# Query features kept in PSUM, groups placed two slots after their sums, one PSUM bank for all placements

## The reference

```python
xn = layernorm(x)
x = x + segment_sum(edge_weight[:, None] * xn[src], dst) @ gnn_W + gnn_b   # 100000 edges
      + linear_attention(xn) @ Wp + bp                                     # q, k = elu(.) + 1, 8 heads
x = x + adaptive_ffn(layernorm(x))        # weights merged from 8 experts by a gate, then a layer norm
```

## Time and profile before

| | us |
|---|---|
| median of 3 runs | 1649.34 (1647.26 to 1649.66) |
| the profiled execution | 1655.24 |
| its span, first to last instruction | 1653.3 |

### The profile page before, as it was taken

One profiled execution on the slowest core, in us unless ns is written; L12 is line 12 of the kernel. 1 busy time (PEld: TensorE's weight loads), 2 busy tenths in 40 slices (PEclk: granted clock), 3 DMA queues, 4 the chain that ended last, 5 costly groups with the idle time before them and its releaser, 6 DMA issues. The chain is left out here.

```text
span 1653.3 us, 27434 instructions
## 1 busy us (share of the span) xinstructions
PE 1478.6 (89%) x8552; PEld 652.4 (39%) x8552; DVE 1148.2 (69%) x2243; ACT 706.1 (43%) x1143; POOL 893.6 (54%) x883
## 2 busy tenths in 40 slices
PE   4988889999999999999999999989986999888995
PEld 2544333333333333434444444434433444543331
DVE  7978545565655655578888888868876666346777
ACT  4777533333333333224333343333335667424443
POOL 1003177777777777767777777777772444100000
PEclk9999989999999999979999999999997999999997
DMA  7899688888888888767777777777776335426674
GB/s 230 290 323 332 229 257 263 259 256 251 258 253 262 258 260 285 240 183 219 223 227 224 234 228 225 224 249 228 218 204 204 154 152 206 146 101 209 229 234 152
DMA packets 163487, 379.44 MB, mean 229 GB/s; under 512 B 26437, under 2 KB 32215, under 8 KB 163363
## 3 DMA queue, kind: packets, MB, share of 16 engines
q0 software_dynamic: 62720, 205.57, 40.9%
q1 hardware_dynamic: 99923, 171.27, 30.0%
q10 hardware_dynamic: 720, 1.06, 0.2%
HBM read 300.77 MB, written 78.23 MB: 229 GB/s over the span
## 5 line engine op out<-in xcount | busy, mean ns | idle before, releaser
L1083 POOL DMA_INDIRECT rows<-y_rows,idxT x516 | 515.7, 999 | 178.4 <-issue 166.8
L1417 DVE SCALAR_TENSOR_TENSOR acc<-bank,maskt,acc 128x512 f32 x392 | 275.8, 745 | 184.8 <-PE bank L1972 141.5
L848 ACT ACTIVATE mb<-bank,ones,ncols 128x512 f32<-128x512 f32 x98 | 76.3, 778 | 374.2 <-PE bank L1861 374.2
L1972 PE MATMUL bank<-part,plc 128*128 128x512 f32 x392 | 213.9, 628 | 0.7 <-ACT part L842 0.7
L842 ACT COPY part<-bank 128x512 f32<-128x512 f32 x196 | 113.0, 577 | 166.1 <-PE bank L1962 166.0
L1861 PE MATMUL bank<-Wg,xtb 128*128 128x512 f16 x588 | 137.1, 384 | 16.4 <-DVE xtb L1354 7.3
L1962 PE MATMUL bank<-rows,hots 128*32 128x512 f16 x1548 | 115.8, 405 | 33.7 <-DMA rows<-y_rows,idxT 32.8
L1861 PE MATMUL bank<-Wk,xta 128*128 128x512 f16 x588 | 139.2, 388 | 0.0
L1861 PE MATMUL bank<-ztg,G 128*128 128x512 f16 (+1 forms) x624 | 136.3, 371 | 0.0
L1861 PE MATMUL bank<-Wq,xta 128*128 128x512 f16 x588 | 136.2, 381 | 0.0
L1861 PE MATMUL bank<-KVP,qT 128*128 128x512 f16 x588 | 136.2, 381 | 0.0
(11 more groups left out here) (314 smaller groups left out, 2418.5 us busy)
## 6 DMA issues: line engine op xcount, KB each, us to landing
xta<-xt_rows SPq DMA_DIRECT2D x98, 256.0 KB, 4.0
x_rows<-xhl SPq DMA_DIRECT2D x49, 256.0 KB, 3.6
xt_rows<-xtb SPq DMA_DIRECT2D x49, 256.0 KB, 3.9
y_rows<-yb SPq DMA_DIRECT2D x49, 256.0 KB, 3.4
xr<-x_rows SPq DMA_DIRECT2D x49, 256.0 KB, 4.1
z_rows<-zn SPq DMA_DIRECT2D x49, 256.0 KB, 2.0
zt_rows<-ztg SPq DMA_DIRECT2D x49, 256.0 KB, 2.0
zq<-z_rows SPq DMA_DIRECT2D x49, 256.0 KB, 2.7
```

The costliest lines, as they stand in the source:

```text
L848: nc.scalar.activation(mb[:, :], of[:, :], ACT.Relu, scale=ncols[:, col:col + 1], bias=ones[:, 0:1]).then_inc(f_min, 1)
L1083: pool.indirect_dma_start(out=row_slot(s, k).rearrange("p a d -> p (a d)"), out_offset=None, in_=y_rows, in_offset=bass.IndirectOffsetOnAx ...
L1417: nc.vector.scalar_tensor_tensor(out=flat(acc, tile + m), in0=placed_bank(s)[:, :], scalar=maskt[:, m, s:s + 1], in1=flat(acc, tile + m), ...
L1972: nc.tensor.matmul(placed_bank(s)[:, :], plc[:, s // WG % 3, s % WG, :], part32[:, s % 2, :], start=True, stop=True).then_inc(placed, 1)
```

## The change

- The query tile's features, their product with the keys' sums and the shares are all written back to the tile's own PSUM bank (`q_bank`); `kf`, `qk` and `qs` are not used there. The product two tiles later waits for the low part of the tile that held the bank (`q_low`).
- Sums alternate between banks 4 and 7, and part(s) waits for the copy of group s-2 (`part_kept`) in place of the additions. All placements use bank 6: place(s) waits until all groups before s are added. place(s-2) stands in slot s, add_group(s-3) too. `part32` has three buffers.
- `plc` is made by one instruction for each group, against `iota16` and a float32 target; the constant `iota128` goes.
- `scales` moves to the head of the fourth tick, in the head and the tail stage.

```diff
-EDGE_BANKS = (6, 7, 4)
+PART_BANKS, PLACED_BANK = (4, 7), 6
...
-SLOTS_END = max(NGR + 2, Q_FIRST + Q_SPACE * (T - 1) + 7)
+SLOTS_END = max(NGR + 3, Q_FIRST + Q_SPACE * (T - 1) + 7)
...
-        tgt = put("tgt", [P, NGR], F16)
+        tgt = put("tgt", [P, NGR], F32)
...
-            return bank[EDGE_BANKS[2 * s % 3]]
+            return bank[PART_BANKS[s % 2]]
 
         def placed_bank(s):
-            return bank[EDGE_BANKS[(2 * s + 3) % 3]]
+            return bank[PLACED_BANK]
...
-                at_least(act, placed, s - 1)
-                nc.scalar.copy(part32[:, s % 2, :], edge_bank(s)[:, :]).then_inc(part_kept, 1)
+                at_least(act, placed, s - 2)
+                nc.scalar.copy(part32[:, s % 3, :], edge_bank(s)[:, :]).then_inc(part_kept, 1)
...
-                nc.scalar.activation(qhl[:, 0, :], qs[:, :], ACT.Copy, scale=QS).then_inc(q_high, 1)
+                nc.scalar.activation(qhl[:, 0, :], q_bank(t)[:, :], ACT.Copy, scale=QS).then_inc(q_high, 1)
...
             def head_tick(g, j):
+                group_work(head, g, j, scales, 3)
                 group_work(head, g, j, first_half, 0)
...
-                nc.vector.tensor_tensor(plc[:, w % 3].rearrange("p g m -> p m g"), iota128[:, :, :],
-                                        tgt[:, WG * w:WG * w + WG].rearrange("p (a g) -> p a g", a=1).broadcast_to([P, P, WG]),
-                                        ALU.is_equal).then_inc(placing, 1)
+                for m in range(WG):
+                    s = WG * w + m
+                    ins = nc.vector.tensor_scalar(plc[:, w % 3, m, :], iota16[:, :], tgt[:, s:s + 1], None, ALU.is_equal)
+                ins.then_inc(placing, 1)
...
-                nc.vector.scalar_tensor_tensor(out=kf[:, 0, :], in0=q_bank(t)[:, :], scalar=cols[:, 2:3], in1=mb[:, :],
+                nc.vector.scalar_tensor_tensor(out=q_bank(t)[:, :], in0=q_bank(t)[:, :], scalar=cols[:, 2:3], in1=mb[:, :],
                                                op0=ALU.mult, op1=ALU.max).then_inc(f_used, 1)
...
-                nc.vector.tensor_tensor(qk[:, :], kf[:, 0, :], ksb[:, :], ALU.mult).then_inc(q_summed, 1)
+                nc.vector.tensor_tensor(q_bank(t)[:, :], q_bank(t)[:, :], ksb[:, :], ALU.mult).then_inc(q_summed, 1)
...
-                nc.vector.tensor_reduce(den[:, :], by_head(qk[:, :]), AX_X, ALU.add).then_inc(q_summed, 1)
+                nc.vector.tensor_reduce(den[:, :], by_head(q_bank(t)[:, :]), AX_X, ALU.add).then_inc(q_summed, 1)
...
-                nc.vector.tensor_tensor(by_head(qs[:, :]), by_head(qk[:, :]),
+                nc.vector.tensor_tensor(by_head(q_bank(t)[:, :]), by_head(q_bank(t)[:, :]),
...
-                nc.vector.scalar_tensor_tensor(out=qhl[:, 1, :], in0=qs[:, :], scalar=QS, in1=qhl[:, 0, :],
+                nc.vector.scalar_tensor_tensor(out=qhl[:, 1, :], in0=q_bank(t)[:, :], scalar=QS, in1=qhl[:, 0, :],
...
-                tile = tile_at_group(s - 2)
-                add_group(s - 2, tile)
+                tile = tile_at_group(s - 3)
+                add_group(s - 3, tile)
...
-                    add_mix(t, 2 * min(s - 1, NGR))
+                    add_mix(t, 2 * min(s - 2, NGR))
...
             def tail_tick(g, j):
+                group_work(tail, g, j, scales, 3)
                 if exists(g, j):
...
-                at_least(pe, edge_added, 2 * (s - 2))
+                at_least(pe, part_kept, s - 1)
...
                 pe.wait_ge(part_kept, s + 1)
+                at_least(pe, edge_added, 2 * s)
                 pe.wait_ge(placing, s // WG + 1)
...
-                pe.wait_ge(f_used, n - 1)
+                if t < 2:
+                    pe.wait_ge(k_summed, T)
+                at_least(pe, q_low, t - 1)
...
-                if s != NGR - 1:
-                    part(s)
-                else:
-                    place(s - 1)
+                part(s)
...
-                if s != NGR - 1:
-                    place(s - 1)
-                else:
-                    part(s)
+                place(s - 2)
```

More of the change, by code:

```diff
@@ L230, in build @@
         wlT = put("wlT", [P, NSG], F16)
-        tgt = put("tgt", [P, NGR], F16)
+        tgt = put("tgt", [P, NGR], F32)
         maskt = put("maskt", [P, 2, NGR], F32)
-        wofff = put("wofff", [1, NGR], F32)
         tileof = put("tileof", [1, NGR], I32)
-        iota128 = put("iota128", [P, P, WG], F16)
         iota32 = put("iota32", [P, W, WS], F16)
@@ L248, in build @@
         KVP16 = over(rV, ("KVP16", [P, 2, C, D], F16))
-        qk, qs, qhl, kvt = over(
-            rA, ("qk", [P, D], F32), ("qs", [P, D], F32), ("qhl", [P, 2, D], F16), ("kvt", [P, C, P], F32))
+        qhl, kvt = over(rA + 8 * D, ("qhl", [P, 2, D], F16), ("kvt", [P, C, P], F32))
         qT = over(rP, ("qT", [P, 2, 2, C, P], F16))
@@ L268, in build @@
             rG, ("xhl", [P, 4, 2, D], F16), ("xtb", [P, 2, 2, C, P], F16), ("yb", [P, 2, 2, D], F16))
+        wofff = over(rG + 32 * D, ("wofff", [1, NGR], F32))
         kf, ksacc, mb, xta, hots, plc, part32 = over(
             rW, ("kf", [P, 2, D], F32), ("ksacc", [P, D], F32), ("mb", [P, D], F32), ("xta", [P, 2, 2, C, P], F16),
-            ("hots", [P, 3, 2, W, WS], F16), ("plc", [P, 3, WG, P], F32), ("part32", [P, 2, D], F32))
+            ("hots", [P, 3, 2, W, WS], F16), ("plc", [P, 3, WG, P], F32), ("part32", [P, 3, D], F32))
         tabu, idxu, hotu, colu, tabcu, whu, wlu = over(
@@ L888, in _ @@
             act.wait_ge(y_low, T)
-            act.wait_ge(pool_set, 21)
+            act.wait_ge(pool_set, 20)
             for s in range(K_FIRST, SLOTS_END):
@@ L1021, in _ @@
                       allow_small_or_imprecise_dtypes=True).then_inc(pool_set, 1)
-            pool.iota(iota128[:, :, :], pattern=[[1, P], [0, WG]], base=0, channel_multiplier=0,
-                      allow_small_or_imprecise_dtypes=True).then_inc(pool_set, 1)
-            pool.wait_ge(pool_set, 16)
+            pool.wait_ge(pool_set, 15)
             for m in (ident, ident16):
@@ L1027, in _ @@
                                    pattern=[[-1, P]], channel_multiplier=1).then_inc(pool_set, 1)
-            pool.wait_ge(pool_set, 18)
+            pool.wait_ge(pool_set, 17)
             for b in range(2):
                 pool.memset(headmask[b * HD:(b + 1) * HD, b * HD:(b + 1) * HD], 1.0).then_inc(pool_set, 1)
-            pool.wait_ge(pool_set, 20)
+            pool.wait_ge(pool_set, 19)
             pool.nop(nofuse=True).then_inc(consts_made, 1)
@@ L1367, in head_tick @@
                         weight_low(k, w16, raw, made, at - KQ_LOW_AT[k - 1], 2)
-                group_work(head, g, j, scales, 3)
                 g2, j2 = back(g, j, 3)
@@ L1476, in q_share @@
                 dve.wait_ge(q_summed, 3 * t + 3)
-                at_least(dve, q_low, t)
-                nc.vector.tensor_tensor(by_head(qs[:, :]), by_head(qk[:, :]),
+                nc.vector.tensor_tensor(by_head(q_bank(t)[:, :]), by_head(q_bank(t)[:, :]),
                                         rden[:, :].rearrange("p (h d) -> p h d", d=1).broadcast_to([P, H, HD]), ALU.mult
@@ L1566, in tile_at_group @@
                 return dve.value_load(tileof[0:1, s:s + 1], min_val=0, max_val=T - 2) if 0 <= s < NGR else None
-            dve.wait_ge(pool_set, 21)
+            dve.wait_ge(pool_set, 20)
             for s in range(K_FIRST, SLOTS_END):
-                tile = tile_at_group(s - 2)
-                add_group(s - 2, tile)
+                tile = tile_at_group(s - 3)
+                add_group(s - 3, tile)
                 if s == TURN + 1:
@@ L1694, in tail_tick @@
                 group_work(tail, g, j, second_half, 1)
-                group_work(tail, g, j, scales, 3)
             row_ticks(dve, tail_tick, T + 1)
@@ L1970, in place @@
                 pe.wait_ge(part_kept, s + 1)
+                at_least(pe, edge_added, 2 * s)
                 pe.wait_ge(placing, s // WG + 1)
-                nc.tensor.matmul(placed_bank(s)[:, :], plc[:, s // WG % 3, s % WG, :], part32[:, s % 2, :],
+                nc.tensor.matmul(placed_bank(s)[:, :], plc[:, s // WG % 3, s % WG, :], part32[:, s % 3, :],
                                  start=True, stop=True).then_inc(placed, 1)
@@ L2113, in _ @@
             pe.wait_ge(mix_added, T)
-            pe.wait_ge(edge_added, 2 * (NGR - 2))
+            pe.wait_ge(part_kept, NGR - 1)
             for f in range(C):
```

2 lines of the change are left out of this document (removed).

## The result

The changed kernel takes **1675.85 us** (median of 3 runs, 1673.52 to 1678.94), the kernel before 1649.34: ratio 1.0166, 95% interval 1.0136 to 1.0195. It is slower, 1.9 us from the forecast of 1674. The profiled execution took 1678.94 us, span 1677.0. In the experiments e2_rest and e3_psum further down one run of six each lay far outside the others (3733.79 and 1905.65 us), and their ratios leave it out.

A forecast was written before the change was run, and what follows sets the result against it. GpSimd's gathers were taken to pace the slots, TensorE right behind. Terms +18 + 12 + 1 + 1 - 5 - 2 = +25 us gave 1680 for the profiled execution, 1674 us as median; range 1643 to 1698.

The forecast's parts named there:

- The handshake: Placements sharing bank 6: each waits for the previous group's additions, so two can't start closer than 2.78 us.
- Query stage: One tight place per query tile, 46 in all, rhythm 10.42 to 10.70 us: +18 us, between +13 and +24.
- The second loop: Query stage: additions queue behind five feature instructions on VectorE and the next product waits, 10.71 us per tile.
- Key stage: Four tight places per 11 slots, 32 of 1.03 us, less gather waits: +12 us, between +2 and +12.6.
- The term that I subtracted: Key stage: 20.4 us of TensorE's waits for gathered rows, taken off the 33 us of new stalls.
- Between keys and queries: Tight slots among serial work from keys to queries: +1 us, at least 0, at most 3.
- End of the stage: Last groups alternate placement and additions, two full intervals of 2.78 us: +1 us, between -2 and +4.
- Scales: Row scales moved to the head of their tick spare ScalarE waits: tail -5 us, head -2 us.
- Features in PSUM: VectorE's query features reading and writing PSUM: 0 us, at worst 0.05 us each and 7 us for the stage.
- (a): Rival, relief: stalls don't show, gathers are no longer held, query tile takes 10.0 us: 1623 us, chance 0.14.
- (b): Rival, even: stalls fall where TensorE lost time anyway and the scales bring -12: 1649 us, chance 0.12.
- (c): Rival, clock: TensorE, standing 1 us some eighty times, is granted a lower clock: 1696 us, chance 0.10.

The follow-up runs named there:

- e2_rest: Changed kernel with only the bank and slot part undone (three rotating banks, placement one slot behind): 1620.40 us.
- e3_psum: Kernel before with only the queries' features in PSUM: 1627.56 us.
- e5: Changed kernel with VectorE's second addition of each group left out: 1621.74 us.
- e6: Changed kernel with a third addition per group, the first one done once more: 1767.13 us.
- e7: Changed kernel with the second query product issued ahead of the placement of its slot, nothing else: 1670.14 us.
- e1: Kernel before with only the bank and slot part, third buffer for kept sums and new placement matrices: 1681.59 us.
- e4: Kernel before with only the row scales moved to the head of their tick in head and tail: 1645.91 us.
- e10: Changed kernel with three rotating banks, but the query's multiplication and share reading two SBUF tiles again: 1639.53 us.

## Why the prediction was right

**The handshake, right.** 1.26 + 1.41 + 0.11 = 2.78 was forecast, 2.77 came, once per query tile and four times in eleven key slots: medians in slots 3, 5, 7 and 9 of the changed kernel, all 2.77. e5 and e6 show that the additions make it, not the copy. From a placement's start to its additions are 1.26 us in both stages, also in the keys, where no features of a query tile stand ahead of them.

**Query stage, +18 against +14.7, inside +13 to +24.** The rhythm was 10.74 on average (median 10.66 = 7.90 + 2.77), forecast 10.70. I had put the slack between two ends; it lay near the lower one: all that TensorE lost per tile before was swallowed, not only the waits that the view of waits names. The second loop does not limit: at 1009.64 the additions waited 0.34 us for the placement, so VectorE was ready earlier than that loop gives it; idle before additions is as short as 0.16 us elsewhere (before, at 728.55), and the tight distance is 2.77 in the keys too, where this loop doesn't exist.

**Key stage, +12 against +6.4, inside +2 to +12.6.** The stalls are as forecast (32.0 us in 34 waits, forecast 33). The term that I subtracted was too small: the waits for gathers are 20.4 us in the view, but eleven slots took 459.2/8 = 57.4 us on average before, where the sum of the undisturbed distances is some 53.9; that is 3.5 for eleven slots and 28 for the stage. The slack should have been read off the distances, as in the queries, and not off the view. Most of what the view leaves out is what came behind a wait: three times in the key stage before, after gathers had been waited for (1.97, 1.93 and 3.55 us), the next products ran slow (pairs of M products 1.06 us in place of 0.59; granted clock 0.83 in the ten microseconds around each), some 1.7 us each by what e6 shows, an estimate; the changed kernel has no such place. And against the other profiles with three banks the growth is 8 to 9 us, nearer the forecast.

**Between keys and queries, +1 against +10.2 (-0.5 and +10.7; 11 to 15 against the other profiles with three banks, 65.7 to 69.8 us from the last key to the third query product and 80.5 here): the step that failed.** I asked there only for tight slots. The rule that I had used for the second loop, that the additions come in VectorE's order behind whatever is before them, applied here to the five microseconds of splitting the matrix and the first features; I didn't follow it. e7 shows 6.6 us of it as the product queued behind the placement; e1 shows that it comes with the bank part.

**End of the stage, +1 against +2.0 (and 1.2 to the tail), in bounds. Scales:** tail -5 against -6.7, and e4 shows it alone: -6.9, ScalarE's waits gone. In the head -2 was forecast; +3.2 is in the table, but profiles with the old order lie at 210.0 to 213.0 and those with the new one at 208.1 to 213.1, so no effect can be told.

**Features in PSUM, 0 in this kernel, right,** and for the reason given: the chain grew by 27 ns in all (744 to 759, 694 to 699, 686 to 691, 691 to 699, 686 to 680 ns in the query stage). The Trainium skill (VectorE: DVE Perf Modes, The TRN2 errata) would have made it 65 ns for each instruction whose source moved to PSUM, an estimate from its cycles; the rows of these runs don't show that, +5, +5, +8 and -6 ns for the four. The page's row is for PSUM to SBUF, which is the form of the fourth alone. With its other rule (SBUF — State Buffer, Who interferes with whom) e10 agrees: 0.949 to 0.992 us per gather and 13 us for two instructions per tile with a second SBUF input.

**The rivals.** (a), relief at 1623 us, is what the change would have brought without the bank: e2 is at 1620.4. The bound given there, a tight distance under about 2.1 us, can be checked too: e5 has 2.10 and 1621.7. (b) didn't come, and neither did (c): the clock of the long stages is 0.99 and 0.98. But (c) was no empty worry: with stands of 1.60 us in place of 0.94, in e6, it cost some 25 us, at 0.97 in both stages. So the terms of the main stages missed by -3 and -6, the unforeseen start by +9; these nearly cancel. The profiled execution came at 1678.94 against 1680, and the offset to the median, carried over as 5.9, was 3.1. Part of the closeness of 1.9 us is luck.

## What to carry to other kernels

A wait between two engines costs what is missing between the two events that it ties together: write down the distances on the waiting engine in every stage, those between the stages too, and compare them with the length of the handshake. Where one distance is too short, moving the instruction behind the next long piece of work can be worth as much as another buffer, as long as nobody's serial chain then queues behind it. A stand can also cost more than its length, when the engine runs slower behind it. A relief of one engine is worth nothing while a new wait paces another, so parts of a change have to be timed alone and together.

## What the runs showed of the hardware

A gather on GpSimd that has started beside a VectorE instruction with two SBUF inputs ends 0.82 us after that instruction does; one PSUM input in its place removes this completely (0.943 us on average in the query stage). VectorE reads and writes PSUM in place at the price of SBUF: 680 to 759 ns for 128x512. After TensorE had stood for 6.92 us its next 128x512 placements and product ran at half speed (2.05 and 4.18 us in place of 1.10 and 2.76), after 3.24 us too (2.05 and 4.48); after 2.36 us in e7 and with some eighty stands of about 0.94 us they didn't, and the granted clock of the stages stayed at 0.98 to 0.99. The length of one stand alone doesn't decide it: in e6 fifteen stands of 1.6 to 2.0 us, of 78 that long, had a stretch at half speed behind them (a product of 4.42 us), and in the kernel before it followed waits of 1.93 and 1.97 us.
